# A conditioned attention and feed-forward block: weights passed transposed, no separate weight stage, feed-forward weights loaded during their own stage

## Reference

```
def rms(x, t, gw, gb, bw, bb):
    g = (t @ gw.T + gb)[:, None, :];  b = (t @ bw.T + bb)[:, None, :]
    return g * x * rsqrt(mean(x * x, -1) + 1e-6) + b
def attention(h):                     # 16 heads of 32
    q, k, v = h @ Wq.T, h @ Wk.T, h @ Wv.T
    return (softmax(q @ k.T / sqrt(32)) @ v) @ Wo.T
def swiglu(h):                        # 2048 hidden units
    return silu(h @ gate_w.T) * (h @ hid_w.T) @ out_w.T
x1 = x + attention(rms(x, t, g1w, g1b, b1w, b1b))
out = x + x1 + swiglu(rms(x1, t, g2w, g2b, b2w, b2b))
```

## Time and profile before

| | |
|---|---|
| median of 3 runs | 2663.32 us (2656.36 to 2665.85) |
| profiled execution | 2667.43 us, its span 2665.6 us |
| setup block | 0.8 to 32.4 us |
| attention program | 32.4 to 1545.6 us |
| feed-forward program | from 1545.6 us; its first product at 1593.7 us |
| mean granted TensorE clock | 0.984 of full |

### The profile page before, as it was taken

How to read it: one execution, slowest core, us unless ns; L and a number is a source line. 1 busy time by engine, 2 the same in 40 slices (tenths; PEclk the granted TensorE clock), 3 DMA queues, 4 the chain that set the end, 5 groups by cost and what they waited for, 6 DMA issues and landing times. The chain is left out here.

```text
span 2665.6 us, 39058 instructions
## 1 busy us (share of the span) xinstructions
PE 2522.3 (95%) x12037; PEld 1695.3 (64%) x12037; DVE 1497.0 (56%) x2349; ACT 1277.5 (48%) x2242; POOL 766.6 (29%) x561
## 2 busy tenths in 40 slices
PE   6999989999989999899999879999999999999999
PEld 5654437544446444365444468888888888888887
DVE  4666745667726667446677245454545454545454
ACT  4356661566653556625566533334334433434343
POOL 0155550455531555514555411010101010101010
PEclk8999999999999999999999979999999999999999
DMA  5211203212132212032121360010101000100000
GB/s 172 66 40 49 55 28 100 48 45 56 44 87 52 45 40 64 28 100 48 37 64 44 127 225 1 9 40 12 38 12 37 14 36 13 36 13 37 16 33 16
DMA packets 66120, 135.21 MB, mean 51 GB/s; under 512 B 13669, under 2 KB 15721, under 8 KB 64617
## 3 DMA queue, kind: packets, MB, share of 16 engines
q1 hardware_dynamic: 64808, 128.24, 16.6%
q0 software_dynamic: 1088, 4.19, 0.5%
HBM read 59.78 MB, written 19.92 MB: 30 GB/s over the span
## 5 line engine op out<-in xcount | busy, mean ns | idle before, releaser
L365 POOL TENSOR_TENSOR sums<-probs 128x512 f32<-128x512 f32 x512 | 653.3, 1301 | 793.2 <-ACT probs L504 791.6
L580 DVE TENSOR_REDUCE pmax<-bank 128x1 f32<-128x512 f32 x1024 | 654.9, 684 | 282.2 <-PE bank L756 271.4
L504 ACT ACTIVATE probs<-bank 128x512 f32<-128x512 f32 x1024 | 584.3, 597 | 402.8 <-PE bank L819 368.6
L819 PE MATMUL bank<-qs,ks 128*128 128x512 f32 x1024 | 458.8, 453 | 29.4 <-ACT probs L504 28.7
L756 PE MATMUL bank<-ks,qs 96*128 96x512 f32 x1024 | 402.9, 406 | 28.1 <-DVE pmax L580 28.1
L819 PEld LDWEIGHTS bank<-qs,ks 128*128 128x128 f32 x1024 | 191.5, 188 | 372.2 <-ACT probs L504 225.1
L1385 PE MATMUL bank<-h_hi,gu_hi 128*128 128x512 f32 x1024 | 399.6, 390 | 6.4 <-DVE gu_lo L1250 3.8
L1385 PE MATMUL bank<-h_lo,gu_hi 128*128 128x512 f32 x1024 | 399.1, 390 | 0.0
L1385 PE MATMUL bank<-h_hi,gu_lo 128*128 128x512 f32 x1024 | 399.0, 390 | 0.0
L1278 DVE TENSOR_TENSOR sg<-bank,sg 128x512 f32<-128x512 f32 x128 | 88.4, 690 | 378.6 <-PE bank L1385 378.6
L779 PE MATMUL bank<-probs,v 128*32 128x512 f32 x2048 | 275.9, 611 | 8.0 <-ACT o L446 5.3
(11 more groups left out here) (119 smaller groups left out, 2911.9 us busy)
## 6 DMA issues: line engine op xcount, KB each, us to landing
ks<-qk_hi SPq DMA_DIRECT2D x136, 128.0 KB, 2.4
qs<-qk_hi SPq DMA_DIRECT2D x264, 64.0 KB, 2.0
x<-in_x SPq DMA_DIRECT2D x10, 1024.0 KB, 5.1
res<-in_x SPq DMA_DIRECT2D x9, 1024.0 KB, 5.2
x<-attn_out SPq DMA_DIRECT2D x9, 1024.0 KB, 7.5
ks<-qk_lo SPq DMA_DIRECT2D x68, 128.0 KB, 2.4
qs<-qk_lo SPq DMA_DIRECT2D x132, 64.0 KB, 2.0
wv<-wv_parts SPq DMA_DIRECT2D x4, 2048.0 KB, 9.5
```

Of the source, the lines that this page charges most:

```text
L365: nc.gpsimd.tensor_tensor(sums[:, h, :], probs[:, 0, h, :], probs[:, 1, h, :], ALU.add) \
L504: nc.scalar.activation(probs[:, s % 2, h, :], sbank[i % SB][:], ACT.Exp, scale=SCALE).then_inc(st_done, 1)
L580: nc.vector.reduce_max(pmax[:, t, h, hf:hf + 1], mbank[n % MB][:], AX_X).then_inc(sq_done, 1)
L819: nc.tensor.matmul(sbank[i % SB][:], ks[:, g % 2, h, s * P:(s + 1) * P], qs[:, u % 3, h, :], start=True, stop=True).then_inc(st_ready, 1)
```

## The change

The host passes all weights transposed and laid out for the partitions. The setup block is gone: its condition products, splits and stores stand in the lead of attention_program. Each attention weight is loaded into the place of its low part and split there by one ScalarE and one VectorE instruction over all 2048 columns (`weight_hi`, `weight_lo`). VectorE writes the constants of `ks` and `mt` before the norm. The feed-forward weights are loaded straight into `wT` (2 slices, 1 MB, per DMA) and `woT` (4 slices, 1 MB, per DMA), 12 DMAs issued at the start of ffn_program; each engine's split of a slice waits for its DMA. The loads that POOL issues in the last batch are now two: the attention output of the first 512 tokens, and their x. Their sums are made by VectorE instead of POOL, and stand behind the split of slice 0 on ScalarE's side.

```diff
 def attention_program(...):
+    raw = [at("wq_raw", [P, KT, D], F32, "wq_lo"), at("wk_raw", [P, KT, D], F32, "wk_lo"),
+           at("wv_raw", [P, KT, D], F32, "probs_lo"), at("wo_raw", [P, KT, D], F32, "wo_lo")]
         # SyncE
-            hold(sp, held, cst["wv_stored"], 16)
-            hold(sp, held, cst["wo_stored"], 16)
+            load_first_x(0)
+            sp.dma_start(small[:], cond_small).then_inc(cond_loaded[0], 16)
+            load_condition(0)
+            load_weight(0)
+            load_first_x(1)
+            load_weight(1)
+            load_weight(2)
+            load_condition(1)
+            load_weight(3)
             stack(None, ("Q", 0), 0)
             stack(None, ("K", 0, NHALF - 1), 0)
+            hold(sp, held, w_lo[2], 1)
+            sp.dma_start(wv_dram, wv[:].bitcast(F32)).then_inc(wv_stored, 16)
+            hold(sp, held, w_hi[3], 1)
+            sp.dma_start(wo_dram, wo[0][:].bitcast(F32)).then_inc(wo_stored, 16)
+            hold(sp, held, wo_stored, 16)
         # GpSimd, last batch
             for n, (place, src) in enumerate(ffn_loads):
-                pool.wait_ge(sq_ready, NB * (NU * NMAX + NT) - NT + 2 * n + 1)
+                pool.wait_ge(sq_ready, NB * (NU * NMAX + NT) - NT + 3 * n + 1)
         # ScalarE
             for t in range(TPH):
                 square(None, 0, t)
+            weight_hi(0)
             act.wait_ge(const_dve, 2)
+            for tile in LEAD_MISC[:KT]:
+                work_tile(None, tile)
             for t in range(TPH):
                 square(None, 1, t)
+            weight_hi(1)
-            for tile in LEAD_MISC:
+            for tile in LEAD_MISC[KT:]:
                 work_tile(None, tile)
+                if tile == ("Q", 0):
+                    weight_hi(2)
+            weight_hi(3)
         # VectorE: constants of ks and mt first, then
+            condition(0)
             mean_square(None, 0)
             for t in range(TPH):
                 scale_x(None, 0, t)
+            weight_lo(0)
+            for tile in LEAD_MISC[:KT]:
+                work_tile(None, tile)
             mean_square(None, 1)
             for t in range(TPH):
                 scale_x(None, 1, t)
-            for tile in LEAD_MISC:
+            weight_lo(1)
+            for tile in LEAD_MISC[KT:]:
                 work_tile(None, tile)
+                if tile == ("Q", 0):
+                    weight_lo(2)
+            weight_lo(3)
+            condition(1)
         # TensorE
+            condition(0)
             for tile in LEAD_MISC:
                 ...
+            condition(1)
+            for s in w_hi, w_lo:
+                pe.wait_ge(s[2], 1)
+            pe.wait_ge(cond_done, 4)
             with pe.Fori(0, NB) as b:

-def attention_setup(...):   # the whole block

+FFN_LOADS = [("gu", 0), ("gu", 2), ("o", 0), ("gu", 4), ("gu", 6), ("gu", 8), ("o", 4), ("gu", 10), ("gu", 12), ("o", 8), ("gu", 14), ("o", 12)]
 def ffn_program(...):
         # SyncE
-            load_tokens(0, 0, 0, None)
-            for n in range(EARLY, len(FFN_LOADS)):
-                ...
+            for kind, j in FFN_LOADS:
+                if kind == "gu":
+                    sp.dma_start(wT[:, j:j + GU_GROUP], gu_w[:, j:j + GU_GROUP]).then_inc(gu_loaded[j // GU_GROUP], 16)
+                else:
+                    sp.dma_start(woT[:, j:j + WO_GROUP, :], out_w[:, j:j + WO_GROUP, :]).then_inc(wo_arrived[j // WO_GROUP], 16)
         # ScalarE
             def gu_hi(j, slot):
+                act.wait_ge(gu_loaded[j // GU_GROUP], 16)
                 ...
-            for i, (kind, n) in enumerate(lead):
-                ...
             gu_hi(0, 0)
+            for t in range(TPH):
+                act.wait_ge(lead_sum, t + 1)
+                square(0, t)
+            act.wait_ge(norm_now, 2)
+            for k in range(KT):
+                norm_tile(k, k, 0, k % GU_BANKS)
         # VectorE
+            for t in range(TPH):
+                nc.vector.tensor_tensor(x1[:, t, :], x1[:, t, :], res[:, 0, t, :], ALU.add).then_inc(lead_sum, 1)
+            mean_square(0)
+            for t in range(TPH):
+                nc.vector.tensor_tensor(res[:, 0, t, :], res[:, 0, t, :], x1[:, t, :], ALU.add).then_inc(lead_sum, 1)
+            scale_x(0)
+            gu_lo(0, 0, 0)
+            for k in range(KT):
+                norm_tile(k, k, k, k, 0, k % GU_BANKS)
         # TensorE
+            pe.wait_ge(x_scaled, TPH)
+            for k in range(KT):
+                transposes(k, k % GU_BANKS)
```

More of the change, by code:

```diff
@@ L785, in _, with condition @@
             pe.sem_inc(d_ready, 1)
+            def condition(i):
+                pe.wait_ge(cond_loaded[0], 32)
+                if i:
+                    pe.wait_ge(cond_loaded[1], 16)
+                for m in (2 * i, 2 * i + 1):
+                    for k in range(KT):
+                        col = (m * KT + k) * NB
+                        last = nc.tensor.matmul(sbank[1][:, col:col + NB], gwT[:, m, k * P:(k + 1) * P], t_T[:],
+                                                start=True, stop=True)
+                last.then_inc(cond_ready, 1)
+            condition(0)
+            pe.wait_ge(id_step, 4)
             for tile in LEAD_MISC:
@@ L1329, in transposes @@
                 last.then_inc(g_ready, 1)
-            for i, (kind, n) in enumerate(lead):
-                if i >= GU_BANKS:
-                    before = lead[i - GU_BANKS]
-                    if before[0] == "t" or before[1] % 2 == 0:
-                        pe.wait_ge(g_act, act_lead(i - GU_BANKS + 1))
-                    if before[0] == "t" or before[1] % 2:
-                        pe.wait_ge(g_dve, dve_lead(i - GU_BANKS + 1))
-                if kind == "t":
-                    if n == 0:
-                        pe.wait_ge(x_scaled, TPH)
-                    transposes(n, i % GU_BANKS)
-                    continue
-                load, c = n // 4, n % 4
-                if load >= EARLY and c == 0:
-                    slot = raw_slot(load)
-                    pe.wait_ge(raw_loaded[slot], 16 * sum(raw_slot(m) == slot for m in range(EARLY, load + 1)))
-                for j in range(4):
-                    last = nc.tensor.transpose(psum[i % GU_BANKS][:, j * P:(j + 1) * P],
-                                               raw[raw_slot(load)][:, j, c * P:(c + 1) * P], ident[:])
-                last.then_inc(g_ready, 1)
-            pe.wait_ge(g_act, NW // 2 + KT)
-            pe.wait_ge(g_dve, NW // 2 + KT)
+            pe.wait_ge(x_scaled, TPH)
+            for k in range(KT):
+                transposes(k, k % GU_BANKS)
+            pe.wait_ge(g_act, KT)
+            pe.wait_ge(g_dve, KT)
             def out_product(b, hf, j):
@@ L1397, in _, with condition_block @@
                     out_product(b, hf, NJ - 1)
-def condition_block(nc, x, t, wq, wk, wv, wo, cond, gate_w, up_w, out_w, out):
+def condition_block(nc, x, cond_small, cond_w, w_in, gu_w, out_w, out):
     attn = nc.dram_tensor("attn_out", (NB, L, D), F32, kind="Internal").ap()
@@ L1444, in condition_block @@
     cst["x_first"] = [at(f"x{hf}", [P, TPH, D], F32, ("x4", "o")[hf]) for hf in range(NHALF)]
-    assert places["h2_hi"] >= places["ks"] + 4 * GH * L and places["h2_lo"] >= places["h2_hi"] + 8 * KT * QB \
-        and places["x1"] <= places["probs"]
-    raw = [at(f"raw{i}", [P, 2, KT, QB], F32, ("h2_hi", "h2_lo")[i]) for i in range(2)]
-    cst["raw"] = [raw[i // 2][:, i % 2, :, :] for i in range(4)]
-    early = [(cst["raw"][raw_slot(n)], weight_source(n, gate_w, up_w, out_w)) for n in range(EARLY)]
+    wT, x1, res = at("wT", [P, NJ, 2, KT, P], F32, "wT"), at("x1", [P, TPH, D], F32, "x1"), at("res", [P, 2, TPH, D], F32, "res")
+    cst["ffn_early"] = wT, x1, res
+    assert places["x1"] >= places["ks"] + 4 * GH * L and places["res"] + 4 * TPH * D <= places["probs"]
+    early = [(x1[:], attn[0, 0:QB, :].rearrange("(t p) d -> p t d", p=P)), (res[:, 0, :, :], x[0, 0:QB, :].rearrange("(t p) d -> p t d", p=P))]
     cst["g1"], cst["b1"], cst["g2"], cst["b2"] = cst["cond"]
```

310 lines of the change are left out of this document (107 added, 203 removed).

## The result

The changed kernel takes 2622.19 us (median of four, 2619.94 to 2624.36), against 2662.27 before: ratio 0.9848, 95% interval 0.9832 to 0.9864. The forecast was 2618.5, with a range of 2606 to 2634. The profiled execution took 2623.54, its span 2621.7, so 43.9 us less than the span before; the sum had 44.9. The medians moved by less, 40.1 us, and the measured one lies 3.7 over the forecast; the profiled execution before (2667.4) lay 5.2 us over its median, the one after 1.4 over its own.

The account below looks back on a forecast made before the run. TensorE, 95% busy, bounds the kernel; only four places where it waits can shrink. 8.1 + 5.6 + 3.8 + 26.6 + 0.8 = 44.9 us off the profiled 2667.4 gives 2622.5, so a median of 2618.5, range 2606 to 2634.

Parts of the forecast that it names:

- Place 1: Program start to first V product: setup gone, tokens loaded first, V at 55.1 us instead of 63.2; gain 8.1.
- Place 2: V stage of batch 0: the hole from waiting for the K stack's DMAs goes; gain 5.6 us, at least 2.
- Place 3: Last batch's output products beside POOL's early loads: fewer loads shorten copies by 2.5 and the next block's start by 1.3; gain 3.8.
- the two thirds: Share taken of the 3.7 us by which the last batch's output copies outlast batch 0's: 2.5 us (0 to 3.7).
- Place 4: Feed-forward lead, SP's first issue to first product: 21.4 us instead of 48.0, as transposes go; gain 26.6 (21 to 28).
- the 0.8: Feed-forward slice 2: the clash that cost TensorE 0.8 us before is counted as gained.
- 1.5 for the low clock: Feed-forward start: 1.5 us allowed for low clock when timing ScalarE's wait and TensorE's need of slice 4.
- No stall: Feed-forward before slice 4: its split ends at 51.5, TensorE wants it at 53.7; only 2 us of cover.
- A: Slow feed-forward weight loads: at 196 GB/s a 29 us stall and 2647, at 290 an 11 us stall and 2630; 13%.
- C: Slower than before: tokens wait behind all weights; at 110 GB/s weights end at 117 and the time is 2699; 4%.
- B: The front gives little: splits or late x0 eat the start-to-V gain and half of batch 0's V-stage gain; 2629.5; 13%.
- D: No overlap: ScalarE waits longer for slice 0's DMA, everything behind it late; 5 us gives 2623.5, 10 gives 2628.5; 5%.

Follow-up runs that it names:

- k_stack_behind_all_stores: Against the changed kernel, SyncE begins both stores (Wv, Wo) only when Wo's high part is done, waits for them, then stacks K; 2630.7 us.
- tensor_kept_busy: Against the changed kernel, 94 extra identity transposes on TensorE in the feed-forward lead (60 while waiting for tokens, 34 before the first product); 2622.58 us.
- squares_first: Against the changed kernel, ScalarE squares the tokens before it splits slice 0 in the feed-forward lead; 2619.8 us.

## Why the prediction was right

**What bounds the kernel** held: beside the four places and the clock, only the batch turns differ. **Place 1** was 1.9 too careful. The order of steps was right to 0.1 us up to the variance; Q came at 29.4 for 29.8, K at 39.4 for 42.0, V at 53.1 for 55.1. The mis-sized terms are the splits over 2048 columns, 1.90 on ScalarE and 2.29 on VectorE where four rows of 512 gave 2.5 each, and Q's 12 matmuls, 3.7 for 5.2, since the clock rose within them.

**Place 2** had the right mechanism (shown by k_stack_behind_all_stores) and the wrong size, 3.0 for 5.6. The wait and its aftermath did go, 40.5 to 34.9; but the sum took V's beginning at full clock. Behind TensorE's pause of 3.8 us before V and the tiny products ahead of it, V's first 5 us ran at the lower clock, and its first evacuation came 2.6 us later. Places 1 and 2 together came to 13.1 for 13.7.

**Place 3** came to 3.1 for 3.8. The bound from batch 0 was sound, the two thirds were a guess; the last batch's copies span 21.3 to 23.4 in 13 profiles, and the 23.2 of before lies inside that, so the 1.4 is not shown to be a gain. The other 1.7, from the last copy to the next program, is: that stretch takes 5.4 and 5.5 in the two kernels with four early loads, and 3.7 in all the others.

**Place 4** came to 25.3 for 26.6 and then lost 2.0 where 0.8 was to be won. The first product is 1.2 late, 0.5 of it by the load (5.3 for 4.8), the rest by small waits. The mis-sized term is the last one of the sum, the 0.8. It counted the old stop as gained and the first products as costing what they did before; "1.5 for the low clock" stood in the cover alone, and was too small there: two slices took 3.1 more than at full clock (1.9 before), and tensor_kept_busy gives back 2.8. "No stall" failed by 1.6 us: the tokens landed at 38 for 40, but both of GpSimd's additions caught the two halves of one split, 10.1 us, where the sum had one meet, 5.7. That step rested on the earlier trace rows, which show one of two such meetings.

**Rivals.** A (slow weights) is refuted by 416 to 426 GB/s, and with it the idea that the rule of the Trainium skill on the row pitch might reach down to this one: "DMA: Bandwidth & Descriptors", section "Latency and other measured facts", has 207 GB/s at 512 KiB, close to its full 214, and the loss at larger pitches, which is in accord with no loss at 64 KB here. C rested on A. B did not occur. D was right in its mechanism though small in its size: the DMA was only 0.5 late, but squares_first shows that standing behind it costs 5.4 us for nothing.

The good hit of the total owes something to luck: the sum for the work of the change is 39.3 of 44.9, and 4.6 came from the turns, which the sum left at nothing. By the medians, 40.1 of 44.8, the miss is in plain view.

## What to carry to other kernels

When loads are moved beside compute, ask first what really needs them: here one split did, and squares_first shows that the squares ahead of it needn't wait. Look next at what else is queued behind these loads, and at the order on the engine that waits first. A price for "the first products" must be taken at the clock that the pause before them leaves. And where an unchanged stretch scatters by 5 to 10 us between executions, compare stage boundaries, not totals, to judge edits of 2 to 5 us.

## What was not expected of the hardware

- 16 matmuls of four columns, 1.84 us of "busy" TensorE, followed by a pause of 0.8 us, did not keep the clock: within 1.6 us of V's start it was at half, and V's first evacuation came 1.5 us later than at full clock.
- A VectorE operation of 0.7 us that begins during GpSimd's addition over 2048 columns lasts until that ends, up to 5 us; one that begins 0.13 us before it is not touched, nor was one with an input in PSUM (0.69 us) in the midst of it.
- Loads of 1 MB with 8 KB per partition out of rows of 64 KB ran at 416 to 426 GB/s, faster than the 388 of the earlier trace rows.
- In a steady stretch in which TensorE was busy 9.0 of 10 us at full clock in one execution, the granted clock was 0.83 in another of the same program. Such falls cost 7.8 and 17.3 us in two profiles.
